# One stage's set-up loads, the last softmax denominators and a first pair of inputs placed elsewhere in a six-stage kernel

## The chip, the cores and the metric

The kernel runs on one core of a Trainium2 chip. The core has TensorE (matrix products into PSUM), VectorE, ScalarE and GpSimd for the rest, and SyncE, which here only issues DMAs. The metric is the device time of one launch in microseconds, the median of several runs.

## The reference

The input is 16 images of 64 channels by 32x32 positions (1024 tokens each), all float32. What is computed, one step after another:

```python
# L0: transformer block per image, 8 heads of 32
qkv = layer_norm(x) @ w_qkv.T
out = softmax(q @ k.T / sqrt(32)) @ v
y   = x + out @ w_proj.T + b_proj
y   = y + relu(layer_norm(y) @ w1.T + b1) @ w2.T + b2
# L1: residual block
z   = relu(bn2(conv3x3(relu(bn1(conv3x3(y, c1))), c2)) + y)
# L2: iterative whitening over groups of 16 channels, all images together
m   = mean(z);  Sigma = EPS*I + (z-m)(z-m).T / n;  P = I
for _ in range(5): P = 1.5*P - 0.5*(P@P@P) @ (Sigma/trace(Sigma))
w   = (P / sqrt(trace(Sigma))) @ (z-m) * weight + bias
# L3: state space model over the 1024 tokens of each image
xi, gate = split(layer_norm(w) @ W_in.T)
u   = silu(causal_conv4(xi));  dt, B, C = split(u @ W_x.T)
d   = softplus(dt @ W_dt.T + b_dt)
h_t = h_{t-1} * exp(d_t * A) + d_t * u_t * B_t;   y_t = h_t . C_t
out = ((y + u*Dp) * silu(gate)) @ W_out.T + w
```

## The kernel before

The kernel is written by hand for each engine: every stage is a block with one program for each of the five engines, ordered by semaphores, and all engines meet at the end of a block. Six blocks follow one another: layer norm (`layer_norm_phase`), attention (`attention_phase`), feed-forward with the two convolutions (`feed_forward_conv_phase`), the whitening matrix (`whitening_phase`), whitening with a second layer norm (`whiten_norm_phase`), and the state space model (`state_space_phase`). Between stages the data goes through DRAM. Two images lie side by side on the 128 partitions (a pair); there are 8 pairs. Each stage has its own SBUF tiles, given back when it ends, and so each loads its own weights, columns of biases and small constant matrices at its start. A column of biases (`for_both_images`) is 64 numbers read twice, one number for each partition.

Layer norm has two rounds of four pairs. SP loads the pairs (line 69) and is done with that when the last buffer of the second round is free; GpSimd stores the results (line 141) and waits for the last store.

Attention goes through 32 groups (16 images by 2 groups of four heads), each in two halves of 512 queries. A half has eight steps, one for each block of 128 keys (`KB` = 8): TensorE makes the scores of four heads (lines 416 and 423), ScalarE takes the exponentials into `probs` (line 527), TensorE multiplies the block before with the values into `O` (`values`, line 435). The denominators are sums of `probs` over the keys. They go another way: SP copies key block 1 into `odd_sums` (`copy_block`, line 306), GpSimd adds blocks 0, 2, 4, 6, 7 in place (`add_even`, line 615) and has accumulating DMAs add blocks 3 and 5 (`add_odd`, line 607) and then the one sum to the other (`add_sums`, line 622), and TensorE adds up the 128 partitions with a matrix of ones (`denominator`, line 408). For all but the last half this is done one half later, in step 14 or 6 of the next one (`extra`). ScalarE takes the reciprocal as Ln and Exp (lines 498, 502) and copies `O` into `att` (line 491), GpSimd multiplies the two (`normalise`, line 627), SP stores (line 298). Behind the last half the same steps stand by themselves, one after another. While a group runs, TensorE and VectorE also make the row maxima of the next one (lines 356, 565); the last group (`"last"`) has none of these to make. `image(b, stage)` is SP's program for one image.

The feed-forward stage runs pairs through a software pipeline. On SP `load(0, 0)` brings the attention output and the input of pair 0 (lines 745, 747) behind two matrices, then come the other weights (lines 751 to 756) and `load(0, 1)`. GpSimd issues the DMAs of 14 columns (lines 991, 993) and clears two padded buffers (line 995). ScalarE and VectorE make the batch-norm factors `bn` from those columns, and only then does ScalarE raise `c1_done`, on which TensorE's first `project` (line 788) waits.

Whitening loads three matrices and waits for them before its first product (line 1051). The stage after it loads four columns and a matrix and waits for all five before its first product (line 1214). The state space stage clears `xn`, loads the first image (line 1352), then eleven constants (lines 1364 to 1374), and waits for all before it makes the combined tap weights (from line 1431 on) and the first convolution (line 1449).

Of the kernel before, what the change touches and what calls it, by code (L numbers as in the profile page):

```python
# [36 lines left out]
def layer_norm_phase(nc, sem, x_d, gain, shift, mean_m, out_d):  # L37
# [3 lines left out]
    with ExitStack() as ctx:  # L41
# [23 lines left out]
        def _(sp):  # L65
# [10 lines left out]
            with sp.Fori(1, ROUNDS) as i:  # L76
                for u in range(FLIGHT):
                    load(i, u)

# [68 lines left out]
def attention_phase(nc, sem, xn_d, wqkvT, ident_bf, attn_d):  # L148
# [65 lines left out]
    def same_bank_before(stage, grp, unit):  # L214
# [8 lines left out]
        return was, grp - 1, [u for u in UNITS[was] if u[3] == unit[3]][-1]  # L223

    with ExitStack() as ctx:
# [61 lines left out]
        def _(sp):  # L287
# [20 lines left out]
            def image(b, stage):  # L308
# [13 lines left out]
                copy_block(b, 1, 1)  # L322
# [4 lines left out]
            with sp.Fori(0, 2) as i:  # L327
                for n in range(NB // 2 - 1):
                    image((NB // 2 - 1) * i + 1 + n, "mid")
            image(NB - 1, "last")  # L330
# [5 lines left out]
        def _(pe):  # L336
# [73 lines left out]

            def scores(stage, grp, par, s):
# [30 lines left out]
            def period(grp, par, stage):  # L442
                for s in range(STEPS):
# [34 lines left out]
        def _(act):  # L478
# [30 lines left out]
            def period(grp, par, stage):  # L509
# [42 lines left out]
        def _(dve):  # L552
# [30 lines left out]
            def period(grp, par, stage):  # L583
                for s in range(STEPS):
# [13 lines left out]
        def _(pool):  # L598
# [30 lines left out]
            def period(grp, par, stage):  # L629
                for half in range(2):  # L630
                    add_even(grp, half, 0)
# [8 lines left out]
                if stage == "last":  # L640
                    normalise(grp, 1)
# [4 lines left out]
def feed_forward_conv_phase(nc, sem, attn_d, x_d, wpT, b_proj, g2, beta2, w1T, b1, w2T, b2, mean_m,  # L646
                            c1, bn1, c2, bn2, out_d, total):

    ROUNDS = PAIRS // 2
    FF = w1T.shape[1]
    M = FF // P  # L660
    PADDED = IMG + 2
    KH = 3
    with ExitStack() as ctx:
        sb = lambda name, shape, dt=F32: ctx.enter_context(nc.sbuf_tensor(name, shape, dt))
        mm = sb("fc_mm", [P, P])
        wp = sb("fc_wp", [P, GROUPS, C])
        w1 = sb("fc_w1", [P, 2, FF])
        w2 = sb("fc_w2", [P, M, C])
        cw = sb("fc_cw", [P, 2, 2 * KH, C])
        cols = sb("fc_cols", [P, 12])  # L670
        b1c = sb("fc_b1c", [P, M])
# [1130 lines left out]
```

## Time and profile before

| | us |
|---|---|
| median of 3 runs | 3499.21 (3495.88 to 3499.93) |
| the profiled execution's own time | 3492.03 |
| its span, first to last instruction | 3490.3 |
| layer norm | 0 to 54.2 |
| attention | 54.2 to 1816.0 |
| feed-forward and convolutions | 1816.0 to 2189.2 |
| whitening matrix | 2189.2 to 2253.7 |
| whitening and norm | 2253.7 to 2328.0 |
| state space | 2328.0 to 3490.3 |

The stages are read off the timeline: each starts where the first DMA or table load of its block is issued. Times inside the kernel count from the span's start. In a row, the second number of a merged piece runs from its first to its last instruction; `[13.75 <-DMA t]` says that the engine had been idle for 13.75 us and what ended it.

### The profile page before, as it was taken

The page shows a single profiled execution, that of the slowest core. Times are in us where ns is not written, and L with a number is a line of the kernel's source. Part 1 is how long each engine was busy: PE and PEld are TensorE (multiplying, and loading weights), DVE is VectorE, ACT ScalarE, POOL GpSimd, SP SyncE. Part 2 cuts the span into 40 slices and gives each one's busy share as a digit, 9 for nine tenths or more (in the row PEclk, how much of TensorE's full clock was granted, in tenths as well). Part 3 has the DMA queues.
Part 4 walks back from the last instruction along what each step waited for, and adds up shares of the span by engine and source line. Part 5 has one row for each costly group of instructions (what it writes and reads, how often), then busy time and mean ns, then how long its engine had stood idle before and what let it go on. Part 6 is the DMA issues. An engine that isn't in the chain of part 4 may idle for free. (4 is left out here: it accounts for less than half of the span.)

```text
span 3490.3 us, 54609 instructions
## 1 busy us (share of the span) xinstructions
PE 3056.1 (88%) x17526; PEld 1156.3 (33%) x17526; DVE 2526.1 (72%) x3282; ACT 2045.6 (59%) x2445; POOL 2163.6 (62%) x876
## 2 busy tenths in 40 slices
PE   5999999999999999999957999556887788877877
PEld 2333333333333333333312333422232222222222
DVE  4888888888788888888812221236898889898888
ACT  3577777777677777777732332235556545655554
POOL 0588888888778888888870000016666766676665
PEclk7899999999999999999979999778999999999999
DMA  3577777777767777777763210134343434434343
GB/s 108 121 170 173 185 170 178 184 172 172 172 168 177 176 179 172 176 185 173 170 149 111 94 42 12 63 116 152 124 154 126 146 129 143 146 127 163 109 158 121
DMA packets 111603, 503.25 MB, mean 144 GB/s; under 512 B 17184, under 2 KB 18276, under 8 KB 78516
## 3 DMA queue, kind: packets, MB, share of 16 engines
q0 software_dynamic: 32704, 218.17, 29.9%
q1 hardware_dynamic: 78676, 282.17, 23.5%
q8 instruction: 132, 2.16, 0.2%
q14 instruction: 91, 0.75, 0.1%
HBM read 192.42 MB, written 39.39 MB: 66 GB/s over the span
## 5 line engine op out<-in xcount | busy, mean ns | idle before, releaser
L565 DVE TENSOR_REDUCE at_pmax<-at_ring 128x1 f32<-128x512 f32 x2048 | 1289.2, 685 | 280.2 <-PE at_ring L356 279.0
L527 ACT ACTIVATE at_probs<-at_sc 128x1024 f32<-128x1024 f32 x1024 | 992.5, 1021 | 371.1 <-PE at_sc L423 369.6
L615 POOL TENSOR_TENSOR at_prob_sums<-at_prob_sums,at_probs 128x2048 f32<-128x2048 f32 x192 | 907.1, 4725 | 72.2 <-ACT at_probs L527 71.9
L416 PE MATMUL at_sc<-at_QT,at_KT 32*128 32x512 f32 x4096 | 774.4, 632 | 8.3 <-issue 7.1
L1695 POOL TENSOR_TENSOR ss_drive<-ss_du,ss_bsb 128x1024 f32<-128x1024 f32 x261 | 610.7, 2353 | 263.4 <-DVE ss_state L1652 256.6
L1595 ACT ACTIVATE ss_decay<-ss_delta,ss_a 128x512 f32<-128x512 f32 x520 | 354.5, 687 | 446.9 <-DVE ss_state L1648 298.9
L435 PE MATMUL at_O<-at_probs,at_V 128*32 128x512 f32 x4096 | 536.2, 607 | 1.1 <-ACT at_probs L527 1.1
L1484 PE MATMUL ss_Y<-ss_seen,ss_ident 128*128 128x512 f32 x1032 | 520.1, 628 | 0.0
L356 PE MATMUL at_ring<-at_KH,at_QH 32*128 32x512 bf16 x2048 | 430.1, 387 | 6.9 <-DVE at_pmax L565 4.0
L1660 DVE TENSOR_TENSOR ss_seen<-ss_state,ss_C 128x1024 f32<-128x1024 f32 x259 | 316.3, 1221 | 78.7 <-PE ss_C L1472 70.8
L1652 DVE TENSOR_TENSOR_SCAN ss_state<-ss_decay,ss_state,ss_drive 128x512 f32<-128x512 f32 x259 | 332.3, 1283 | 33.6
L615 POOL TENSOR_TENSOR at_prob_sums<-at_probs 128x2048 f32<-128x2048 f32 x64 | 299.0, 4671 | 88.0 <-ACT at_probs L527 87.7
L1648 DVE TENSOR_TENSOR_SCAN ss_state<-ss_decay,ss_drive 128x512 f32<-128x512 f32 x259 | 314.9, 1216 | 32.2 <-POOL ss_drive L1695 16.5
L1472 PE MATMUL ss_C<-ss_bc,ss_select 96*128 96x512 bf16 x518 | 160.8, 393 | 191.6 <-DVE ss_seen L1660 191.2
L356 PEld LDWEIGHTS at_ring<-at_KH,at_QH 32*128 32x128 bf16 x2048 | 145.9, 92 | 523.8 <-DVE at_pmax L565 374.6
L423 PE MATMUL at_sc<-at_nrow,at_ones_bf 1*128 1x512 bf16 x2048 | 315.6, 379 | 0.2 <-ACT at_nrow L485 0.2
L1484 PEld LDWEIGHTS ss_Y<-ss_seen,ss_ident 128*128 128x128 f32 x1032 | 201.8, 200 | 228.0 <-issue 174.9
L416 PEld LDWEIGHTS at_sc<-at_QT,at_KT 32*128 32x128 f32 x4096 | 258.6, 184 | 36.9 <-ACT at_probs L527 25.4
L999 POOL DMA_DIRECT2D scratch_x<-fc_out x8 | 4.3, 534 | 345.1 <-ACT fc_out L900 345.1
L607 POOL DMA_DIRECT2D at_odd_sums<-at_probs x128 | 120.5, 941 | 149.3 <-DMA at_odd_sums<-at_probs 95.1
L369 PE MATMUL at_ring<-at_xn,at_w 64*128 64x512 f32 x256 | 150.3, 668 | 27.0 <-DMA at_xn<-scratch_xn 19.4
L1472 PEld LDWEIGHTS ss_C<-ss_bc,ss_select 96*128 96x128 bf16 x518 | 40.4, 101 | 385.9 <-DVE ss_seen L1660 323.2
(195 smaller groups left out, 2847.7 us busy)
## 6 DMA issues: line engine op xcount, KB each, us to landing
ss_bsb<-scratch_rows SPq DMA_DIRECT2D x265, 512.0 KB, 6.9
at_odd_sums<-at_probs POOLq DMA_DIRECT2D x128, 1024.0 KB, 7.6
at_odd_sums<-at_probs SPq DMA_DIRECT2D x64, 1024.0 KB, 4.8
at_prob_sums<-at_odd_sums POOLq DMA_DIRECT2D x64, 1024.0 KB, 8.1
scratch_attn<-at_att SPq DMA_DIRECT2D x64, 256.0 KB, 2.0
fc_att<-scratch_attn SPq DMA_DIRECT2D x32, 512.0 KB, 5.8
ss_xn<-scratch_xm SPq DMA_DIRECT2D x34, 256.0 KB, 5.6
at_xn<-scratch_xn SPq DMA_DIRECT2D x32, 256.0 KB, 6.5
```

The source lines that it names most:

```text
L356: nc.tensor.matmul(ring[:, unit[3], :], QH[head(h), p, blk(quad // 2)], KH[head(h), p, hs(quad % 2)], start=True, stop=True).then_inc(max_ ...
L416: nc.tensor.matmul(sc[:, h, :], KT[head(h), par, blk(kb)], QT[head(h), par, hs(half)], start=True, stop=False)
L423: m = nc.tensor.matmul(sc[:, of, :], ones_bf[row, :], nrow[row, half, :], start=False, stop=True)
L435: m = nc.tensor.matmul(O[head(h), :], V[:, par, kb, head(h)], probs[:, kb, h, :], start=(kb == 0), stop=(kb == KB - 1))
L527: nc.scalar.activation(probs[:, kb, two, :].rearrange("p h q -> p (h q)"), sc[:, two, :].rearrange("p h q -> p (h q)"), ACT.Exp, scale=SCA ...
L565: nc.vector.tensor_reduce(pmax[:, quad // 2, h, quad % 2:quad % 2 + 1], ring[:, unit[3], :], AX_X, ALU.max, negate=True).then_inc(max_done, 1)
L615: nc.gpsimd.tensor_tensor(prob_sums[:, half, :, :], before, probs[:, POOL_ADDS[n], :, :], ALU.add).then_inc(pool_sums, 1)
L1484: m = nc.tensor.matmul(Y[:, hs(h)], ident[:], seen[:, n % DEPTH, hs(h)], start=False, stop=(n == N - 1))
L1595: nc.scalar.activation(decay[:, hs(h)], delta[:, par, hs(h)], ACT.Exp, scale=a_neg[:, n:n + 1])\
L1652: nc.vector.tensor_tensor_scan(now[:, hs(1)], decay[:, hs(1)], drive[:, n % DEPTH, hs(1)], now[:, HALF - 1:HALF], ALU.mult, ALU.add).then_ ...
L1660: nc.vector.tensor_tensor(seen[:, n % DEPTH, :], state[:, n % 2, :], Cp[:], ALU.mult).then_inc(seen_done, 1)
L1695: nc.gpsimd.tensor_tensor(drive[:, n % DEPTH, :], du[:, par, :], bsb[:, n % SLOTS, :], ALU.mult).then_inc(drive_done, 1)
```

## The change

- A new class `Constants` holds the weights, columns and matrices of all later stages in tiles that live for the whole kernel, with six semaphores. Its `load` (43 DMAs) runs on SP at the end of layer norm's SP program. The loads at the start of the four later stages are gone; their waits now name the new semaphores. Matrices that two stages use (`mean_m`, `ident`) are loaded once.
- SP, before the last image of attention, fetches pair 0 of the feed-forward stage (four DMAs of attention output and one of input, 512 KB each) into tiles of its own. The feed-forward stage begins with `load(0, 1)`.
- In the last half of attention, TensorE sums each key block of `probs` itself: four products with the ones matrix for each of 8 blocks, accumulated in a free PSUM slot (`last_denominators`), one block a step from the second step on and the last block behind the last `values`. The copy, GpSimd's four adds and the three accumulating DMAs of that half are gone, and so is the separate denominator. ScalarE's copy of `O` is gone too: VectorE multiplies `O` in PSUM with the reciprocal. GpSimd's `normalise` of the half before comes at once.
- ScalarE raises `c1_done` before it waits for the columns.

```diff
+class Constants:
+    def load(self, sp):
+        sp.dma_start(self.wp[:], a["L0_conv_w_proj"].rearrange("(g p) c -> p g c", p=P)).then_inc(self.ff_matrices, DMA)
+        sp.dma_start(self.mm[:], a["mean_m"]).then_inc(self.ff_matrices, DMA)
...
+        for n, v in enumerate(vectors):
+            sp.dma_start(self.cols[:, n:n + 1], for_both_images(v)).then_inc(self.ff_vectors, DMA)
...
+        sp.dma_start(self.select[:], a["select_m"]).then_inc(self.ss, DMA)
@@ layer_norm_phase, SP
             with sp.Fori(1, ROUNDS) as i:
                 for u in range(FLIGHT):
                     load(i, u)
+            later.load(sp)
@@ attention_phase
+    LAST_SLOT = (unit_of("last", "den", 0)[3] + 1) % SLOTS
@@ SP
-                copy_block(b, 1, 1)
+                if stage != "last":
+                    copy_block(b, 1, 1)
...
+            for half in range(2):
+                sp.wait_ge(att_stored[half], 2 * GROUPS * DMA)
+            for b in range(2):
+                for g in range(GROUPS):
+                    sp.dma_start(later.att0[:, b, g, :], av[b, g]).then_inc(later.pair0, DMA)
+            sp.dma_start(later.x0[:], x_d[0:2].rearrange("b c s -> (b c) s")).then_inc(later.pair0, DMA)
             image(NB - 1, "last")
@@ TensorE
+            def last_denominators(grp, k):
+                if k == 0:
+                    pe.wait_ge(max_done, counted_before(N_MAX, grp) + N_MAX["last"])
+                    pe.wait_ge(extra_done, unit_count("last", grp, unit_of("last", "turn", 1)))
+                for h in range(GH):
+                    m = nc.tensor.matmul(ring[head(h), LAST_SLOT, :], ones[:, head(h)], probs[:, k, h, :],
+                                         start=(k == 0), stop=(k == KB - 1))
+                if k == KB - 1:
+                    m.then_inc(extra_ready, 1)
...
+                    if stage == "last" and s > KB:
+                        last_denominators(grp, s - KB - 1)
...
                     values(stage, grp, par, 1, KB - 1)
-                    pe.wait_ge(max_done, counted_before(N_MAX, grp) + N_MAX["last"])
-                    pe.wait_ge(extra_done, counted_before(N_EXTRA, grp) + N_EXTRA["last"])
-                    denominator(0, 2 * NG - 1, 1)
+                    last_denominators(grp, KB - 1)
@@ ScalarE
-                    take_raw(grp, 1)
-                    reciprocal(0, counted_before(N_EXTRA, grp) + N_EXTRA["last"] + 1, 2 * NG - 1)
+                    reciprocal(LAST_SLOT, counted_before(N_EXTRA, grp) + N_EXTRA["last"] + 1, 2 * NG - 1)
@@ VectorE
+                if stage == "last":
+                    dve.wait_ge(pv_done, STEPS * NG)
+                    dve.wait_ge(rden_done, 2 * NG)
+                    dve.wait_ge(att_stored[1], (NG - 1) * DMA)
+                    nc.vector.tensor_tensor(att[:, 1, :], rden[:], O[:], ALU.mult).then_inc(od_free, 1)
@@ GpSimd
+                    if stage == "last" and half:
+                        normalise(grp, 0)
+                        continue
@@ feed_forward_conv_phase, SP
-            sp.dma_start(wp[:], wpT.rearrange("(g p) c -> p g c", p=P)).then_inc(first_in, DMA)
-            sp.dma_start(mm[:], mean_m).then_inc(first_in, DMA)
...
-            load(0, 0)
...
             load(0, 1)
@@ ScalarE
+            act.sem_inc(c1_done, 4)
+            act.wait_ge(later.ff_vectors, later.N_FF_VECTORS * DMA)
...
             act.wait_ge(bn_done, 2)
-            act.sem_inc(c1_done, 4)
@@ GpSimd
-            for n, v in enumerate(vectors):
-                pool.dma_start(cols[:, n:n + 1], for_both_images(v)).then_inc(vectors_in, DMA)
...
@@ whiten_norm_phase, TensorE
-            pe.wait_ge(consts_in, 5 * DMA)
@@ state_space_phase, SP
-            sp.dma_start(w_in[0:C, :], w_inT).then_inc(w_in_done, DMA)
             sp.wait_ge(cleared, 1)
             load_x(0)
-            sp.dma_start(cw[:], conv_w).then_inc(consts_in, DMA)
...
```

## Rows read from the trace of the kernel before

**Rows 1.** The page's costliest group: out<-in, count | busy us, mean ns | idle before, releaser.
```profile
L565 DVE TENSOR_REDUCE at_pmax<-at_ring 128x1 f32<-128x512 f32 x2048 | 1289.2, 685 | 280.2 <-PE at_ring L356 279.0
```
**Rows 2.** Timeline, end of attention: start, length, engine, line, operation, tiles, [idle before].
```profile
1790.24 1.94 ACT L527 ACTIVATE at_probs<-at_sc 128x1024 f32<-128x1024 f32 x2
...
1799.94 0.86 POOL L622 DMA_DIRECT2D at_prob_sums<-at_odd_sums  x1 [0.61 <-POOL at_prob_sums L615]
...
1807.04 1.94 PE L408 MATMUL at_ring<-at_prob_sums,at_ones 128*32 128x512 f32 x8 [13.75 <-DMA at_prob_sums<-at_odd_sums]
...
1810.44 1.25 POOL L627 TENSOR_TENSOR at_att<-at_att,at_rden 128x512 f32<-128x512 f32 x1 [9.64 <-ACT at_rden L502]
...
1811.72 0.33 SPq L298 DMA_DIRECT2D scratch_attn<-at_att  x1
```
**Rows 3.** Timeline, start of the feed-forward stage.
```profile
1815.99 1.28 ACT L851 ACT_TABLE_LOAD   x1 [5.70 <-PEq L225]
...
1827.08 8.04 POOL L995 MEMSET fc_pad<- 128x4624 f32 x2
...
1838.41 0.29 ACT L855 ACTIVATE fc_bn<-fc_cols,fc_eps 128x1 f32<-128x1 f32 x1 [21.14 <-DMA fc_b1c<-in_L_conv_b]
...
1840.17 5.79 PE L788 MATMUL fc_A<-fc_att,fc_wp 128*64 128x512 f32 x16 [31.20 <-ACTq L859]
```
**Rows 4.** Timeline of TensorE in the last half of attention.
```profile
1776.46 1.15 PE L416 MATMUL at_sc<-at_QT,at_KT 32*128 32x512 f32 x8
...
1777.75 1.06 PE L435 MATMUL at_O<-at_probs,at_V 128*32 128x512 f32 x8
...
1787.80 1.04 PE L408 MATMUL at_ring<-at_prob_sums,at_ones 128*32 128x512 f32 x8
1788.77 1.15 PE L416 MATMUL at_sc<-at_QT,at_KT 32*128 32x512 f32 x8
```
**Rows 5.** Windows: length, busy time and count by engine, PE clock, DMA share, GB/s.
```profile
1691.00:1717.00 26.00, 25.80 (x218) 9.83 (x216) 21.66 (x36) 19.38 (x23) 20.92 (x9) 1.00 0.71 163
...
1773.00:1777.00 4.00, 4.00 (x24) 0.92 (x26) 0.00 (x0) 1.17 (x2) 3.53 (x2) 0.59 1.06 324
...
1837.00:1844.00 7.00, 3.83 (x10) 1.39 (x12) 0.87 (x6) 0.88 (x4) 0.00 (x0) 0.50 0.97 369
```
**Rows 6.** Timeline around the half before which the change puts its fetch.
```profile
1692.95 0.47 SPq L306 DMA_DIRECT2D at_odd_sums<-at_probs  x1
...
1721.16 0.87 POOL L622 DMA_DIRECT2D at_prob_sums<-at_odd_sums  x1 [0.61 <-POOL at_prob_sums L615]
...
1733.75 1.04 PE L408 MATMUL at_ring<-at_prob_sums,at_ones 128*32 128x512 f32 x8
```
**Rows 7.** Timeline, starts of the three later stages.
```profile
2189.21 1.28 ACT L1086 ACT_TABLE_LOAD   x1 [5.86 <-PEq L663]
...
2192.15 0.59 PE L1051 MATMUL wh_small<-total,wh_pair 128*128 128x1 f32 x2 [11.40 <-DMA wh_ident<-in_ident]
...
2253.68 0.61 SPq L1192 DMA_DIRECT2D wn_cols<-in_L_conv_weight  x1
...
2259.53 9.51 PE L1214 MATMUL wn_bank<-x_centred,wm 128*128 x16 [7.32 <-DMA wn_mean_m<-in_mean_m]
...
2329.06 1.13 SPq L1352 DMA_DIRECT2D ss_xn<-scratch_xm  x2
...
2340.51 0.69 PE L1431 MATMUL ss_aux<-ss_ident,ss_w_in 64*128 64x64 f32 x2 [30.43 <-DMA ss_ident<-in_ident]
...
2345.00 6.00 PE L1449 MATMUL ss_aux<-ss_xn,ss_w_taps 128*128 128x512 f32 x8 [0.96 <-ACT ss_w_taps L1566]
```
**Rows 8.** Tile `ss_xn`, from issue to landing.
```profile
DMA to landing us min/median/max: 3.7/5.6/6.5
```
**Rows 9.** SP's timeline, its last issue in layer norm.
```profile
20.89 0.33 SPq L69 DMA_DIRECT2D ln_x<-in_x  x1
```
**Rows 10.** Tile `fc_w`, its issues on SP: ns min/median/max, first and last start.
```profile
L751 SPq DMA_DIRECT2D fc_w<-in_L_conv_w x2: 1980/2456/2933, 1823.1 to 1826.1; - x2
```

More of the change, by code:

```diff
@@ L41, in layer_norm_phase @@
+def layer_norm_phase(nc, sem, x_d, gain, shift, mean_m, out_d, later):
     with ExitStack() as ctx:
@@ L145, in _, with attention_phase @@
                         pool.sem_inc(xn_free, 2)
-def attention_phase(nc, sem, xn_d, wqkvT, ident_bf, attn_d):
+def attention_phase(nc, sem, xn_d, wqkvT, ident_bf, attn_d, x_d, later):
     NG = NB * GROUPS
@@ L639, in period, with feed_forward_conv_phase @@
                     add_sums(grp, half)
-                if stage == "last":
-                    normalise(grp, 1)
             image_loop(pool, period)
-def feed_forward_conv_phase(nc, sem, attn_d, x_d, wpT, b_proj, g2, beta2, w1T, b1, w2T, b2, mean_m,
-                            c1, bn1, c2, bn2, out_d, total):
+def feed_forward_conv_phase(nc, sem, attn_d, x_d, out_d, total, later):
     ROUNDS = PAIRS // 2
-    FF = w1T.shape[1]
-    M = FF // P
+    M = later.M
     PADDED = IMG + 2
@@ L674, in feed_forward_conv_phase @@
         acc = sb("fc_acc", [P, 2])
-        att = sb("fc_att", [P, 2, 2, GROUPS, S])
-        x = sb("fc_x", [P, 2, S])
+        att = (later.att0, sb("fc_att1", [P, 2, GROUPS, S]))
+        x = (later.x0, sb("fc_x1", [P, S]))
         y = sb("fc_y", [P, 2, S])
@@ L697, in feed_forward_conv_phase @@
                                      "conv2_done", "res_done", "out_done", "out_free", "total_done"))
-        in_sem = [sem(f"fc_in{u}") for u in range(2)]
+        in_sem = [later.pair0, sem("fc_in1")]
         stored = [sem(f"fc_stored{u}") for u in range(2)]
@@ L764, in _ @@
             pe.sem_inc(proj_done, 2)
-            pe.wait_ge(first_in, 2 * DMA)
+            pe.wait_ge(later.ff_matrices, later.N_FF_MATRICES * DMA)
             def statistics(dst, src, u, done):
@@ L842, in _ @@
                 stage(0, 0)
-            pe.wait_ge(consts_in, N_MATRICES * DMA)
             pe.wait_ge(cleared, 6)
@@ L989, in _ @@
             pool.sem_inc(out_free, 2)
-            for n, v in enumerate(vectors):
-                pool.dma_start(cols[:, n:n + 1], for_both_images(v)).then_inc(vectors_in, DMA)
-            for m in range(M):
-                pool.dma_start(b1c[:, m:m + 1], b1[m * P:(m + 1) * P].rearrange("(p o) -> p o", o=1)).then_inc(vectors_in, DMA)
             for pad in (pad1, pad2):
@@ L1001, in _, with whitening_phase @@
                     pool.sem_inc(out_free, 1)
-def whitening_phase(nc, sem, x_d, total, pair_m, mask_m, ident_m, centred, wm):
+def whitening_phase(nc, sem, x_d, total, centred, wm, later):
     NC, ITERATIONS = 16, 5
@@ L1049, in _ @@
         def _(pe):
-            pe.wait_ge(consts_in, 3 * DMA)
+            pe.wait_ge(later.whitening, later.N_WHITENING * DMA)
             nc.tensor.matmul(small[:, 0:1], pm[:], total[:], start=True, stop=True).then_inc(mean_sum, 1)
@@ L1161, in _, with whiten_norm_phase @@
             dve.wait_ge(dve_step, 10 + 4 * ITERATIONS)
-def whiten_norm_phase(nc, sem, x, wm, weight, bias, ln_w, ln_b, mean_m, xw_d, xn_d):
+def whiten_norm_phase(nc, sem, x, wm, xw_d, xn_d, later):
     ROUNDS = PAIRS // FLIGHT
@@ L1190, in _ @@
         def _(sp):
-            for n, v in enumerate((weight, bias, ln_w, ln_b)):
-                sp.dma_start(cols[:, n:n + 1], for_both_images(v)).then_inc(consts_in, DMA)
-            sp.dma_start(mm[:], mean_m).then_inc(consts_in, DMA)
             for dst in (xw_d, xn_d):
@@ L1234, in _ @@
             nc.vector.memset(eps[:], EPS).then_inc(eps_set, 1)
-            dve.wait_ge(consts_in, 5 * DMA)
+            dve.wait_ge(later.norm, later.N_NORM * DMA)
             with dve.Fori(0, ROUNDS) as i:
@@ L1427, in _ @@
         def _(pe):
-            pe.wait_ge(consts_in, 11 * DMA)
-            pe.wait_ge(w_in_done, DMA)
+            pe.wait_ge(later.ss, later.N_SS * DMA)
             nc.tensor.matmul(aux[:, 0:C], w_in[0:C, 0:DI], ident[0:C, 0:C], start=True, stop=True).then_inc(plain_ready, 1)
@@ L1568, in _ @@
                     .then_inc(taps_done, 1)
-            act.wait_ge(consts_in, 11 * DMA)
+            act.wait_ge(later.ss, later.N_SS * DMA)
             take_x(0)
@@ L1626, in _ @@
             nc.vector.memset(xn[:], 0.0).then_inc(cleared, 1)
-            dve.wait_ge(consts_in, 11 * DMA)
+            dve.wait_ge(later.ss, later.N_SS * DMA)
             dve.sem_inc(y_step, 1)
```

160 lines of the change are left out of this document (86 added, 74 removed).

## The prediction

> **What bounds the kernel now.** The profiled execution took 3492.03 us, its span is 3490.3, so 1.7 lie around it; the median of the runs is 3499.21, 7.2 above. The sum below is made against 3492.03 and the 7.2 are added at the end. A measurement of this kernel can tell about 0.2% (7 us) from no change.
>
> I read the stages off the timeline, then each seam between two stages: when the stage begins, when its first product starts, and what that product's row names as the end of its wait. Inside the long stages the change touches only the last half of attention. So the question is what stands on the path at five seams and in one half of 26 us.
>
> At the end of attention the last exponential ends at 1790.24 + 1.94 = 1792.18, but the last store is only issued at 1811.72. In between stand GpSimd's add chain up to the DMA at 1799.94, a wait of 13.75 us on TensorE for that DMA, 1.94 us of denominators, 1.46 us to the multiply on GpSimd, and 1.25 us for that [rows 2]. The next stage begins at 1815.99 and its first product at 1840.17, 24.18 us later: ScalarE had waited 21.14 us for the last column, and TensorE waits for ScalarE's `c1_done` [rows 3]. All other engines are idle there but for GpSimd's two memsets. Whitening's first product starts 2.94 us after its table load and is released by a matrix; the stage behind it waits 5.85 us (2253.68 to 2259.53) for a matrix queued behind four columns; the state space stage makes its first convolution 15.94 us after it issued its input [rows 7].
>
> **The change part by part.**
>
> *End of attention.* Removed: 1811.72 - 1792.18 = 19.54 us from the last exponential to the issue of the last store [rows 2]. In its place: the last `values` (1.06) and the last block's denominators. One set of four such products costs 1.04 [rows 4]; the row counts them as x8, so a block's four products are one such piece. Then Ln and Exp, 1.46 with the hand-offs by the old chain; then the multiply. VectorE multiplying 512 columns of PSUM is not in the trace; its row maximum over as many takes 0.685 [rows 1], GpSimd's multiply 1.25 [rows 2], and I take 0.7, the same engine and memory. Hand-offs 0.3, and `values` may start some 0.6 late, since block 6's denominators stand ahead of it in TensorE's order. Sum 0.6 + 1.06 + 1.04 + 1.46 + 0.7 + 0.3 = 5.2. Gain 14.3.
>
> *What it costs the half.* TensorE gets seven more pieces of about 1.0 in steps 9 to 15. From step 11 to step 15 scores start at 1776.46 and 1788.77, 12.31 us for four steps, 3.08 a step, of which the old denominators take 1.04 once. A step's own work is 1.29 for scores (1776.46 to 1777.75) and about 1.0 for values [rows 4], 2.3 in all; the rest is waiting for exponentials, which the new piece partly fills. With it a step is 3.3, and the one with the old denominators too 4.3: 14.2 instead of 12.3, +1.9. ScalarE's reciprocal in step 14, which held up the last exponentials by 0.8, is covered then (-0.8). Just before, from 1773 to 1777, the granted clock is 0.59 of the full 2.4 GHz, so part of the stretch ran at 1.2 GHz, after TensorE had run out of row maxima to make; that costs 4 x 0.41 = 1.6 [rows 5]. The added products fill that hole; whether the clock then stays up the trace of before cannot show, so the stretch is worth -1.6 to +2 (two new pieces at half the clock). I take +0.4. Together +1.5, bounds -0.5 to +4. The seam of attention gains 14.3 - 1.5 = 12.8.
>
> GpSimd's adds of that half and SP's copy cost nothing off the path and gain nothing.
>
> *The fetch.* Five DMAs (2.6 MB) go on SP's queue ahead of the last image's first copy. That copy is issued at 1692.95 [rows 6], when the exponentials it needs are there; SP has waited for them till then, and five issues of 0.33 [rows 2] fit. The transfers are the question. In that half the DMA engines are 0.71 busy at 163 GB/s; at their fullest they moved 369 GB/s [rows 5], so 2.6 MB are 7.1 us of all engines, and the copy, on the same queue, lands up to that much later. GpSimd's first accumulating DMA waits for the copy, and behind it in GpSimd's order stand two adds, `normalise` and the sum. Of the sum TensorE has this slack: issued 1721.16, read 1733.75, 12.6 us [rows 6] against a landing of 7.1 (1799.94 to 1807.04, [rows 2]): 5.5, of which I count 4.5, since more is in flight there. GpSimd idles some 5 us of the half (20.92 busy of 26, [rows 5]) and so absorbs part of the delay. I take +0.5, bounds 0 to +4 from 7.1 less the slack, with a point for a second victim.
>
> The Trainium skill, "DMA: Bandwidth & Descriptors", section "Issuing engines are not separate DMA queues", says that DMAs from all engines run on the same 16 DMA engines and interleave, so GpSimd's accumulating DMAs would be slowed too, not only the copy on SP. Rows 5 agree in so far as both kinds make up the 0.71.
>
> *Start of the feed-forward stage.* Everything that the first product reads is there; what it still waits for is ScalarE's `c1_done`, behind a table load of 1.28 [rows 3]. So it starts 1.4 after the stage's start instead of 24.18: gain 22.8. What may be late next: the batch-norm factors, 1.8 us from ScalarE's first step to the product (1838.41 to 1840.17), now beside the product; and GpSimd's memsets of 8.04 [rows 3], which stood behind the 14 columns and now begin at once. What they clear is waited for behind the product (5.79) and the chain of five passes over 1024 columns to the normalised pair, each over 1 us by twice the 0.685 of [rows 1]: 1.4 + 5.79 + 5 = 12, so they stay covered. The clock is low before and after: 5.79 for the first product either way. An unseen wait for instructions could appear; bounds 20 to 23.
>
> *The three later seams.* Whitening: 2.94 becomes about 0.3, gain 2.6. The next: the product still waits for ScalarE's `ln_done`, behind the table load, 1.4 in place of 5.85: gain 4.4. State space: issue of the input stays where it is (it waits for a memset). It lands 0.6 (second issue) + 5.6 [rows 8] = 6.2 later; the tap weights took 4.5 from their first product (2340.51 to 2345.00) and stay under it. So 15.94 - 6.2 = 9.7; with a landing of 3.7 it is 11.6, with 6.5 it is 8.8 [rows 7, 8]. The rows' landings are mostly from the loop, with more in flight, so I take 4.6 and 10.7. Together 17.7, bounds 14 to 19.
>
> *The 43 loads.* SP has nothing to issue from 21.2 [rows 9] to the seam at 54.2, 33 us, less the 1 it needs at the barrier. A column of this form on SP's queue took 0.61 to issue [rows 7], and there are 16; the plain ones lie between 0.33 [rows 2] and, behind full queues, 2.93 [rows 10]. 16 x 0.61 + 27 x 0.6 = 26 us: covered. With the two first weight matrices at 2.9 each and 0.9 for the columns it is 35, +3. I take +0.5, bounds 0 to +6, also for layer norm's last stores, which share the engines.
>
> The Trainium skill, same page, "Rules for kernel authors", speaks against these columns: an outermost dimension of two copies keeps a DMA on at most two engines, and transfers under 64 KB are mostly overhead. Here 14 columns, issued by GpSimd, were in at 1838.41, 22.4 us after the stage began [rows 3], with all other loads of the stage beside them; 16 at that pace are 26 us, inside the 33.
>
> *Sum.* -12.8 + 0.5 - 22.8 - 17.7 + 0.5 = -52.3. 3492.0 - 52.3 = 3439.7; in the frame of the median 3446.9. I forecast **3447**.
>
> **The rivals.**
>
> (a) *The fetch holds up attention.* The sums of two halves come late: the one issued beside the fetch and the one behind the copy. Each reaches TensorE 7.1 - 4.5 = 2.6 late, and the delay is not made up: about +5 to +8, 3454. For it: DMA 0.71 busy. Against: GpSimd's idle time.
>
> (b) *The added products run at the lower clock.* If the clock falls as at 1773 in most of the half, eight pieces cost 1.0 more each: +8, 3455. Against: they make TensorE busier.
>
> (c) *SP is late at layer norm's end*: 43 loads at 0.9, 39 us, +6: 3453.
>
> (d) *The seams keep another wait.* The first products find something the rows hide behind the DMA wait, such as code not yet fetched; it costs some 3 to 5 us at each of four seams, half of the gain at the two big ones at most: +15, 3462.
>
> (e) *Slower: the 43 loads stop SP.* All issues on SP are in order and attention cannot begin before the last one. If each went at the pace of the weights behind a full queue, 2.93 at most [rows 10], SP would end at 21.2 + 126 = 147 and attention begin 94 us late: 3447 + 94 = 3541. It decides from a pace of (32 + 52.3)/43 = 2.0 us a load on. For it: two of the rows 10 pace are among them. Against: those stood behind 2.6 MB, and the column on SP took 0.61.
>
> (f) *It doesn't do what it says*: the seams wait as long, because the new semaphores are reached as late as the old; that would need the loads to be in flight 1750 us after their issue. Less than 1%.
>
> **How the numbers follow.** Forecast 0.57; (a) 0.13, (b) 0.09, (c) 0.10, (d) 0.07; (e) 0.02; between them a loss of some 46 us from several of these, within 0.2%: 0.02. Faster 0.96, same 0.02, slower 0.02. The range: the sum's better ends (12.8 + 2, 23, 19, no other cost) give -57, 3442; a run in the frame of the profiled execution is a few us lower, so 3438. Upwards (a), (b) and (c) one at a time reach 3455 and the bounds of two terms together 3461; (d) and (e) are left out.
>
> **What would show it.** Attention's last store issued about 5 us after the last exponential, and that exponential 1 to 2 us later in its half; the feed-forward stage's first product 1.4 after its table load; 0.3, 1.4 and some 5 at the other seams; layer norm's length unchanged at 54.2; TensorE's read of the sum at its place in the half of the fetch. The prediction is wrong if a seam keeps its length with another releaser, if the last half grows by more than 4 us, or if attention begins after 60.

## The result and the profile after

| | before | after |
|---|---|---|
| median, us | 3497.55 (3493.19 to 3499.93) | 3446.18 (3440.86 to 3447.96) |
| profiled execution, us | 3492.03 | 3445.46 |
| ratio | | 0.9852 (0.984 to 0.9864) |

The change saves 51.4 us in the medians and 46.6 in the two profiled executions. By stage, in the profiled ones (a stage of after starts with its first instruction of any engine, since with the loads gone its first DMA or table load can come up to 1.2 us later):

| stage | before | after | difference | forecast |
|---|---|---|---|---|
| layer norm | 54.2 | 53.5 | -0.7 | +0.5 |
| attention | 1761.8 | 1754.2 | -7.6 | -12.3 |
| feed-forward | 373.2 | 354.2 | -19.0 | -22.8 |
| whitening matrix | 64.5 | 62.3 | -2.2 | -2.6 |
| whitening and norm | 74.3 | 69.8 | -4.5 | -4.4 |
| state space | 1162.3 | 1149.8 | -12.5 | -10.7 |
| sum | | | -46.5 | -52.3 |

**End of attention** (timeline of after; it answers to [rows 2]). The last exponentials end at 1800.08 + 1.02 = 1801.10, the last store is issued at 1805.21: 4.1 us where 19.54 were. What is left is values, one block of denominators, Ln, Exp and VectorE's multiply of 0.69.

```profile
1800.08 1.02 ACT L620 ACTIVATE at_probs<-at_sc 128x1024 f32<-128x1024 f32 x1
1801.15 1.07 PE L528 MATMUL at_O<-at_probs,at_V 128*32 128x512 f32 x8 [0.24 <-ACT at_probs L620]
1802.04 1.04 PE L499 MATMUL at_ring<-at_probs,at_ones 128*32 128x512 f32 x8
1803.14 0.60 ACT L591 ACTIVATE at_lden<-at_ring 128x512 f32<-128x512 f32 x1 [2.04 <-PE at_ring L499]
1803.77 0.63 ACT L595 ACTIVATE at_rden<-at_lden 128x512 f32<-128x512 f32 x1
1804.49 0.69 DVE L690 TENSOR_TENSOR at_att<-at_rden,at_O 128x512 f32<-128x512 f32 x1 [39.12 <-ACT at_rden L595]
1805.21 0.33 SPq L373 DMA_DIRECT2D scratch_attn<-at_att  x1
1807.72 1.28 ACT L917 ACT_TABLE_LOAD   x1 [3.32 <-PEq L300]
```

**The half of the fetch** (timeline of after, then two windows with the columns of [rows 5], then two windows of before that lie as far behind the same store, then the landings of tile `at_odd_sums` in after; before: [rows 6]).

```profile
1693.00 1.80 SPq L411 DMA_DIRECT2D k_att<-scratch_attn  x4
1694.84 0.57 SPq L412 DMA_DIRECT2D k_x<-in_x  x1
1695.62 0.48 SPq L381 DMA_DIRECT2D at_odd_sums<-at_probs  x1
...
1711.45 0.88 POOL L704 DMA_DIRECT2D at_odd_sums<-at_probs  x1 [8.10 <-ACT at_probs L620]
...
1732.42 0.88 POOL L719 DMA_DIRECT2D at_prob_sums<-at_odd_sums  x1 [0.61 <-POOL at_prob_sums L712]
...
1740.35 1.94 PE L491 MATMUL at_ring<-at_prob_sums,at_ones 128*32 128x512 f32 x8 [3.74 <-DMA at_prob_sums<-at_odd_sums]
...
1696.00:1702.00 6.00, 5.80 (x52) 1.83 (x46) 5.09 (x10) 4.03 (x6) 4.73 (x3) 1.00 1.01 358
1702.00:1708.00 6.00, 6.00 (x52) 2.00 (x52) 4.92 (x9) 4.12 (x6) 1.35 (x1) 1.00 1.04 289
...
1693.00:1699.00 6.00, 5.80 (x50) 2.01 (x44) 5.11 (x9) 4.03 (x6) 4.37 (x3) 1.00 0.88 259
1699.00:1705.00 6.00, 6.00 (x53) 2.03 (x56) 4.99 (x9) 4.11 (x5) 3.78 (x3) 1.00 0.98 199
...
DMA to landing us min/median/max: 4.4/7.4/15.3
```

The DMA engines are full for 12 us. Before, they were nearly full there too, at fewer GB/s (0.88 and 0.98 busy), which the mean of 0.71 over the half hides. The copy issued at 1695.62 takes 15.3 us to land (5.2 before), GpSimd stands 8.10 us ahead of its accumulating DMA (1.35 us busy in the second window; the row names the exponentials, but the copy that it also waits for landed at 1695.62 + 15.3 = 1710.9), and TensorE now waits 3.74 us for the sum, for which it had not waited before. Behind that wait its granted clock is 0.50, and the product that waited takes 1.94 us instead of 1.04.

**Start of the feed-forward stage** (TensorE's timeline of after, its first three windows of 7 us, and the same three windows of before; before: [rows 3]). The first product starts 1.43 us after the table load, as forecast. But it takes 6.51 us, not 5.79, the third piece 3.62, where before it took 1.98, and the first two hidden products 3.75 and 2.98 (before 3.59 and 1.88): the granted clock of these stretches is 0.58, 0.90 and 0.74, where before it was 0.69, 1.00 and 0.79.

```profile
1809.15 6.51 PE L855 MATMUL fc_A<-k_att,k_wp 128*64 128x512 f32 x16 [6.07 <-ACT L917]
...
1821.58 3.62 PE L836 MATMUL fc_A<-fc_sq,k_mm 128*128 128x512 f32 x4 [2.46 <-ACT fc_sq L929]
1829.68 3.75 PE L875 MATMUL fc_B<-fc_yn,k_w 128*128 128x512 f32 x4 [4.49 <-DVE fc_yn L1011]
1833.23 2.98 PE L875 MATMUL fc_A<-fc_yn,k_w 128*128 128x512 f32 x4
1836.04 1.88 PE L875 MATMUL fc_B<-fc_yn,k_w 128*128 128x512 f32 x4
...
1809.12:1816.12 7.00, 6.51 (x16) 1.94 (x16) 1.36 (x9) 0.78 (x4) 6.51 (x2) 0.58 0.99 346
1816.12:1823.12 7.00, 3.53 (x6) 1.36 (x7) 2.17 (x2) 1.06 (x1) 0.00 (x0) 0.90 0.74 232
1823.12:1830.12 7.00, 2.51 (x4) 0.80 (x3) 2.04 (x2) 2.17 (x2) 0.00 (x0) 0.74 0.40 164
...
1840.14:1847.14 7.00, 5.79 (x16) 1.73 (x16) 1.05 (x1) 0.00 (x0) 0.00 (x0) 0.69 0.53 214
1847.14:1854.14 7.00, 3.97 (x8) 1.35 (x8) 1.45 (x2) 1.36 (x2) 0.00 (x0) 1.00 0.77 265
1854.14:1861.14 7.00, 2.85 (x4) 1.33 (x5) 2.04 (x2) 1.86 (x2) 0.00 (x0) 0.79 0.28 112
```

**Later seams and layer norm's end** (timeline of after; before: [rows 7, 9]). Two of the first products start with their stage, the convolution 6.0 us after its own. SP's last load ends at 51.88, and attention begins at 53.53.

```profile
51.44 0.44 SPq L105 DMA_DIRECT2D k_select<-in_select_m  x1
53.53 1.14 SPq L364 DMA_DIRECT2D at_w<-in_L_conv_w_qkv  x2
...
2161.97 0.56 PE L1108 MATMUL wh_small<-total,k_pair 128*128 128x1 f32 x2 [7.37 <-PEq L750]
...
2224.18 1.28 ACT L1271 ACT_TABLE_LOAD   x1 [20.14 <-PEq L1071]
...
2224.57 2.07 PE L1266 MATMUL wn_bank<-x_centred,wm 128*128 x2 [1.86 <-ACTq L1273]
...
2293.93 0.66 PE L1456 MATMUL ss_aux<-k_ident,k_w_in 64*128 64x64 f32 x2 [17.04 <-PEq L1224]
...
2299.99 1.22 PE L1474 MATMUL ss_aux<-ss_xn,ss_w_taps 128*128 128x512 f32 x1 [1.95 <-DMA ss_xn<-scratch_xm]
```

### The profile page after: what moved, and what is told of

Its sections match the earlier page's. It is cut to its first block and busy times, and to the rows that moved or that the text cites. A ratio compares the mean times of both kernels' runs of the same rounds, so it can differ in the third digit from the quotient of the medians.

```text
span 3443.8 us, 54701 instructions
## 1 busy us (share of the span) xinstructions
PE 3065.5 (89%) x17582; PEld 1159.7 (34%) x17582; DVE 2526.9 (73%) x3283; ACT 2045.1 (59%) x2444; POOL 2132.9 (62%) x854
## 5 line engine op out<-in xcount | busy, mean ns | idle before, releaser
L712 POOL TENSOR_TENSOR at_prob_sums<-at_prob_sums,at_probs 128x2048 f32<-128x2048 f32 x189 | 891.0, 4714 | 70.0 <-ACT at_probs L620 69.6
L1620 ACT ACTIVATE ss_decay<-ss_delta,k_a 128x512 f32<-128x512 f32 x520 | 354.5, 687 | 446.7 <-DVE ss_state L1673 298.7
L1509 PE MATMUL ss_Y<-ss_seen,k_ident 128*128 128x512 f32 x1032 | 520.1, 628 | 0.0
L1497 PE MATMUL ss_C<-ss_bc,k_select 96*128 96x512 bf16 x518 | 160.7, 393 | 191.6 <-DVE ss_seen L1685 191.2
L1509 PEld LDWEIGHTS ss_Y<-ss_seen,k_ident 128*128 128x128 f32 x1032 | 201.7, 200 | 227.9 <-issue 173.1
L1497 PEld LDWEIGHTS ss_C<-ss_bc,k_select 96*128 96x128 bf16 x518 | 40.4, 101 | 385.9 <-DVE ss_seen L1685 323.1
```

Source lines behind the costliest of these rows:

```text
L712: nc.gpsimd.tensor_tensor(prob_sums[:, half, :, :], before, probs[:, POOL_ADDS[n], :, :], ALU.add).then_inc(pool_sums, 1)
L1509: m = nc.tensor.matmul(Y[:, hs(h)], ident[:], seen[:, n % DEPTH, hs(h)], start=False, stop=(n == N - 1))
L1620: nc.scalar.activation(decay[:, hs(h)], delta[:, par, hs(h)], ACT.Exp, scale=a_neg[:, n:n + 1])\
```

## The experiments

Times are medians; the ratio is to the kernel before on the same chip. In all that follows "stretch" is the time from the issue of the store ahead of the last image (1692.41 in after) to the first exponential of the last half (1774.46): 77.09 before, 82.05 after. "Late fetch" is the third experiment, the base of all behind it but the old denominators, whose base is after.

**No fetch.** The five DMAs go back to the start of the feed-forward stage.

```diff
-            for b in range(2):
-                for g in range(GROUPS):
-                    sp.dma_start(later.att0[:, b, g, :], av[b, g]).then_inc(later.pair0, DMA)
-            sp.dma_start(later.x0[:], ...).then_inc(later.pair0, DMA)
...
+            load(0, 0)
             load(0, 1)
```

> The changed kernel without the fetch in attention; pair 0 is loaded at the start of the feed-forward stage, ahead of pair 1. If the fetch is what makes TensorE wait 3.7 us for the sum of the half behind it, the stretch from the store before the fetch to the first exponential of the last half is 77.1 us again, as before the change, instead of 82.1. The first product of the feed-forward stage then waits for 2.6 MB: 7.1 us at 369 GB/s and 2 to 3 of latency, so it starts some 9.5 after the stage's start instead of 1.4. Together +3: 3449. Rival, the stretch is longer for another reason (the profiled execution, the tiles' places): it stays at 82 and the time is 3454.

3447.4 us (3442.36 to 3448.08), 0.9852 (0.9835 to 0.9868). The stretch is 77.27, as before the change: the fetch did cost the 5 us. The first product starts 9.6 us after the stage's start, held by `k_x`:

```profile
1811.96 6.10 PE L849 MATMUL fc_A<-k_att,k_wp 128*64 128x512 f32 x16 [14.25 <-DMA k_x<-in_x]
```

So in its place the fetch gained 8.2 at the one end and lost 5.0 at the other; the medians with it and without it (3446.18 and 3447.4) can't be told apart.

**Fetch behind the copy.** The same five DMAs, issued right behind the first copy of the last image.

```diff
                 copy_block(b, 0, 0)
+                if stage == "last":
+                    fetch()
...
```

> The fetch one step later on SP: behind the last image's first copy instead of ahead of it. If the delay comes from the order on SP's queue (the copy lands 15.3 us after its issue because 2.6 MB stand ahead of it), the copy lands in about 5, GpSimd's first accumulating DMA is not held up, the stretch is 77 to 78 and the time 3441. If it comes from the shared DMA engines, the accumulating DMAs land late in its place, GpSimd's chain is late all the same, the stretch is 80 to 82 and the time 3444 to 3446.

3439.34 us (3432.64 to 3440.03), 0.9827 (0.981 to 0.9843); the stretch is 81.12, so going behind the copy took back only 1 us of the 5. The copy now lands in 5.7 us. GpSimd's timeline shows where the rest stays: its first accumulating DMA goes out in time, but lands after 16.0 us (8.3 before the change), and the second waits for it.

```profile
1721.19 0.88 POOL L708 DMA_DIRECT2D at_odd_sums<-at_probs  x1 [8.92 <-DMA at_odd_sums<-at_probs]
```

So in both places what was in flight beside the 2.6 MB was slowed, SP's copy in after and GpSimd's DMA here. The Trainium skill says in "DMA: Bandwidth & Descriptors", section "Issuing engines are not separate DMA queues", that DMAs of all issuing engines run on the same 16 DMA engines and interleave, and this row agrees (8.92 us of waiting). That the total is 7 us below that of after comes mostly from elsewhere. In the profiled runs the feed-forward stages, of the same code, differ by 5.5 us (349.0 against 354.5 from table load to table load), at granted clocks of 0.75, 1.00, 0.76 and 1.00 in the first four stretches of 7 us instead of 0.58, 0.90, 0.74 and 0.62.

**Late fetch.** The five DMAs go out behind the store of the last image's first group (`store(b, 0, 1)`), into the last half, which has no copy and no accumulating DMAs of its own any more.

```diff
                 store(b, 0, 1)
+                if stage == "last":
+                    fetch()
...
```

> The fetch in the last half of attention, behind the last image's third store, where the copy and the accumulating DMAs of that half are gone. Theory: only one accumulating DMA (the sum of the half before) is in flight beside it, and it has 14 us; the stretch is 77, the last half as in the changed kernel (24.7 from the first to the last exponential's start), the data is there before the stage starts, the time 3441. Rival: the sum lands behind the fetch, up to 7 us late, and TensorE waits 0 to 3 for it; or the fetch lands after the stage's start; time 3442 to 3446.

3437.64 us (3435.49 to 3441.54), 0.9826 (0.981 to 0.9842). The stretch is 76.75, the last half as in after (24.70), the first product 1.43 after the stage's start. The fetch has both ends of its gain here.

**Old denominators.** In after, the last half makes its denominators over SP, GpSimd and DMAs again.

```diff
-                if stage != "last":
-                    copy_block(b, 1, 1)
+                copy_block(b, 1, 1)
...
-                    last_denominators(grp, KB - 1)
+                    denominator(0, 2 * NG - 1, 1)
```

> The changed kernel with the old way of the last half's denominators: copy, GpSimd's adds, accumulating DMAs, then the separate products, and GpSimd's multiply. By the traces the new way gains 17.2 us from the last exponential's start to the stage's end and costs 0.9 in the half: without it the time is 16 longer, 3462. The prediction's terms (14.3 less 1.5) give 3459.

3461.58 us (3457.81 to 3464.21), 0.9894 (0.9878 to 0.9911): 15.4 above after. TensorE's row has its old wait again (13.75 before), in spite of everything else being changed, and the last half is back at 23.77 us from its first to its last exponential, as before (24.70 in after).

```profile
1817.27 1.94 PE L490 MATMUL at_ring<-at_prob_sums,at_ones 128*32 128x512 f32 x8 [15.75 <-DMA at_prob_sums<-at_odd_sums]
```

**TensorE kept busy.** The low clock at the start of the feed-forward stage has two possible causes: the idle time around it, or the work itself. From here on the kernel with the late fetch gets extra products whose results nobody reads, made from a constant of the state space stage; TensorE waits for that constant once, at the start of attention.

```diff
                     last_denominators(grp, KB - 1)
+                    for _ in range(18):
+                        nc.tensor.matmul(ring[:, (LAST_SLOT + 1) % SLOTS, :], ones_bf[0:96, :], later.filler, start=True, stop=True)
...
+            pe.wait_ge(later.ss, later.N_SS * DMA)
...
-            for stage in (project, means, variances):
+            fill(4)
+            for stage, n in ((project, 5), (means, 9), (variances, 16)):
                 stage(0, 0)
+                fill(n)
```

> The kernel with the late fetch (3437.6), with 52 extra bf16 products on TensorE whose results nobody reads, put where it idles: 18 behind the last denominators of attention, 4 at the start of the feed-forward stage, 5, 9 and 16 behind the first three products of pair 0. The feed-forward stage of the late fetch took 351.8, its first product 5.20 and the first two hidden products 3.75 and 3.13 against 3.6, 1.88 and 1.88 at full clock. Theory (the idle stretch at the seam lowers the granted clock, and that gave back part of the 22.8): the granted clock of the first 28 us is 1.0, these three pieces take their full-clock times, stage 346 to 348, time 3433. Rival 1 (the lower clock comes of the pair's own load, not of the idle time before): pieces as before, stage 352, time 3438. Rival 2 (the extra products stand in the way of the pair's own, because at the lower clock they outlast the gaps): stage 355 or more, time 3441 or more.

3430.1 us (3428.77 to 3432.33), 0.9811 (0.9798 to 0.9825): the lowest median of all, though the interval of its ratio overlaps that of the late fetch. The stage takes 344.0 instead of 351.8. TensorE's rows, and the window of the first product; ahead of them the first product with the late fetch, and last the final convolution of the stage, with the late fetch and here:

```profile
1804.64 5.20 PE L859 MATMUL fc_A<-k_att,k_wp 128*64 128x512 f32 x16 [6.10 <-ACT L921]
...
1802.97 3.65 PE L863 MATMUL fc_A<-k_att,k_wp 128*64 128x512 f32 x16 [0.22 <-ACT L931]
...
1819.01 1.95 PE L883 MATMUL fc_B<-fc_yn,k_w 128*128 128x512 f32 x4 [1.04 <-DVE fc_yn L1025]
...
1802.94:1809.94 7.00, 6.69 (x26) 2.47 (x27) 2.32 (x9) 0.78 (x4) 6.52 (x2) 1.00 0.97 346
...
2135.15 12.22 PE L847 MATMUL fc_B<-fc_pad,k_cw 128*64 128x512 f32 x48 [2.46 <-DVE fc_pad L1031]
...
2127.38 10.52 PE L851 MATMUL fc_B<-fc_pad,k_cw 128*64 128x512 f32 x48 [2.46 <-DVE fc_pad L1041]
```

The same product that took 5.20 to 6.59 us takes 3.65 at the full clock, granted at 1.00 through the first four stretches of 7 us. So the idle time lowers the clock, not the work. Of the 7.8 us that the stage is shorter, 4.6 lie in pair 0: its fourth hidden product starts 22.7 us after the stage's start instead of 27.2. The other 3.2 lie in the last pair, some 310 us later, where both kernels have the same code and no extra products: its two convolutions take 11.97 and 10.52 us instead of 13.53 and 12.22. That the extra products have a part in this is not shown; the clock there differs between runs without them too.

**The extra products at the seam alone**, and **in the pair alone**: two halves of the same edit, each shown against the run before.

```diff
-            for stage, n in ((project, 5), (means, 9), (variances, 16)):
+            for stage, n in ((project, 0), (means, 0), (variances, 0)):
```

> The kernel that keeps TensorE busy (3430.1, feed-forward stage 344.0 against 351.8 with the late fetch), with the extra products at the seam alone: 18 behind the last denominators and 4 at the start of the stage, none inside pair 0. If the idle 6 us of the seam lowered the clock: first product 3.65 in place of 5.20, hidden products 1.9 to 2, stage 345 to 347, time 3431. If the pair's own gaps (1.46, 2.46 and 4.49) did it: first product 3.65, but the hidden products behind the last gap 3.75 and 3.1 as with the late fetch, stage 349 to 350, time 3435.

```diff
-                    for _ in range(18):
+                    for _ in range(0):
...
-            fill(4)
```

> The other half: the extra products of pair 0 (5, 9 and 16) without those at the seam. If the seam's idle stretch lowered the clock: first product 5.2 to 6.5, then the clock comes back within the pair, since TensorE is busy, hidden products 1.9, stage 346 to 349, time 3433. If the pair's own gaps did it: only the first product is slow or not even that, stage 345 to 346, time 3431.

At the seam alone: 3435.75 us (3434.53 to 3437.38), 0.9826 (0.981 to 0.9843), stage 351.4. The first product takes 3.65, but the clock falls behind it, and what was won is lost again (the fourth hidden product starts 27.0 us into the stage):

```profile
1802.73 3.65 PE L863 MATMUL fc_A<-k_att,k_wp 128*64 128x512 f32 x16 [0.22 <-ACT L931]
1807.84 1.99 PE L844 MATMUL fc_B<-fc_y,k_mm 128*128 128x512 f32 x4 [1.46 <-DVE fc_y L1014]
1812.29 3.58 PE L844 MATMUL fc_A<-fc_sq,k_mm 128*128 128x512 f32 x4 [2.46 <-ACT fc_sq L943]
1820.36 3.75 PE L883 MATMUL fc_B<-fc_yn,k_w 128*128 128x512 f32 x4 [4.49 <-DVE fc_yn L1025]
```

In the pair alone: 3434.5 us (3431.65 to 3434.95), 0.9823 (0.9806 to 0.9839), stage 346.6. Here the first product is slow, with 0.50 granted in the 1.4 us before it, and all behind it runs at full clock:

```profile
1802.70 6.13 PE L863 MATMUL fc_A<-k_att,k_wp 128*64 128x512 f32 x16 [6.10 <-ACT L930]
...
1821.21 1.95 PE L883 MATMUL fc_B<-fc_yn,k_w 128*128 128x512 f32 x4 [1.04 <-DVE fc_yn L1024]
```

So both idle stretches lower the clock, the one of the seam for the first product, the pair's own gaps for what follows. What each is worth is not shown. The fourth hidden product starts 25.2 us into the stage here, and in the five profiles whose stage has the code of after (after, fetch behind the copy, late fetch, old denominators, sixteen more loads) anywhere from 25.8 to 30.1: only both together, at 22.7, stand well clear. The other 3.1 us of this stage's 5.2 lie in the last pair again, and the ratio is that of the late fetch. The Trainium skill, "TensorE: Matmul & The Clock Gate", section "HAM oscillation — how this bites in real kernels", tells of a kernel whose waits (there for DMAs) between bursts of products drop the clock, so that each burst starts slow; the rows at the seam alone agree, with waits of 1.46 and 2.46 us for VectorE and ScalarE ahead of a product of 3.58 us that took 1.98 with the late fetch.

**Sixteen more loads** at the end of layer norm.

```diff
+        for n in range(16):
+            sp.dma_start(self.more[:, n:n + 1], for_both_images(vectors[n % 12])).then_inc(self.norm, DMA)
...
```

> The kernel with the late fetch, with 16 more columns loaded on SP at the end of layer norm into a tile that nobody reads. Theory (SP's issues now end layer norm, with 1 us of slack at most): the columns cost 16 x 0.98 (14 of them took 13.5 us) = 15.7, attention begins 14 to 16 us later, at 69 to 71, time 3452. Rival (layer norm is still ended by its last store and the loads have room): attention begins at 55, time 3438.

3453.54 us (3448.31 to 3454.27), 0.9873 (0.9857 to 0.9888), 15.9 above the late fetch. Attention begins at 68.35 instead of 55.13, right behind SP's last load:

```profile
67.13 0.43 SPq L108 DMA_DIRECT2D k_select<-in_select_m  x1
68.35 1.14 SPq L367 DMA_DIRECT2D at_w<-in_L_conv_w_qkv  x2
```

That last load moved by 14.06 (53.07 to 67.13), 0.88 a load, and attention by 13.2: the 43 loads left about 0.8 us.

**Columns in the stage.** GpSimd issues the 14 columns at the start of the feed-forward stage, as before; `c1_done` stays early.

```diff
...
+            later.columns(pool)
             for pad in (pad1, pad2):
```

> The kernel with the late fetch, with the 14 columns issued by GpSimd at the start of the feed-forward stage as in the kernel before; everything else (weights, matrices, the early c1_done) as it was. Theory (the gain of 22.8 is of the columns being there; raising c1_done early only lets the first product run): the first product starts 1.4 after the stage's start, but the addition behind it waits for the batch-norm factors, which follow the last column at 15 to 22 us after the start instead of running at 6.7: stage 351.8 + 9 to 15, time 3447 to 3453. Rival (raising c1_done early is what gave the gain, the columns are needed later): at most +3, time 3441.

3449.0 us (3448.0 to 3449.81), 0.9863 (0.9848 to 0.9878). The first product starts at 1.4, but its reader, the addition, starts at 1818.93, 22.2 us after the stage's start, behind the last column:

```profile
1817.33 0.29 ACT L929 ACTIVATE fc_bn<-k_cols,fc_eps 128x1 f32<-128x1 f32 x1 [19.27 <-DMA k_b1c<-in_L_conv_b]
...
1818.93 1.28 DVE L1007 SCALAR_TENSOR_TENSOR fc_y<-fc_A,k_cols,k_x 128x1024 f32<-128x1024 f32 x1
```

The stage takes 371.0, 19.2 more than with the late fetch, where 9 to 15 had been expected. (The medians lie only 11.4 apart; in the profiles this run's attention is 4.5 us shorter and its state space stage 5.7, with code that is the same.) Raising `c1_done` early hides the product under the columns, and no more.

**`c1_done` late.** ScalarE raises it behind the batch-norm factors; the columns stay in layer norm.

```diff
-            act.sem_inc(c1_done, 4)
             act.wait_ge(later.ff_vectors, later.N_FF_VECTORS * DMA)
...
             act.wait_ge(bn_done, 2)
+            act.sem_inc(c1_done, 4)
```

> The kernel with the late fetch, but ScalarE raises c1_done behind the batch-norm factors as in the kernel before; the columns are loaded in layer norm. Theory (with the columns there the factors take 1.4 us): the first product starts 2.8 after the stage's start instead of 1.4, time 3439. Rival (the place of c1_done carries the gain): the product starts 10 us or more later, time 3448 or more.

3436.28 us (3433.17 to 3441.27), 0.9829 (0.9814 to 0.9844), not to be told from the late fetch. The product starts 3.05 us after the stage's start instead of 1.43. With the columns there, the place of `c1_done` is worth 1.6 us at most; the columns carry the rest.

## Why the prediction was right, and where its steps were not

The forecast of 3447 is within 1 us of the median, but its sum was 5.8 us too good against the profiled executions, for which it was made: 3439.7 against 3445.46. It was 4.7 short in attention and 3.8 in the feed-forward stage, and did better by 1.2 in layer norm and 1.5 at the later seams. That the median came out all the same is luck: the 7.2 us added for it belong to the profiled run of before; that of after lies only 0.7 below its median. The steps, one by one:

*End of attention, -14.3.* From the last exponential to the store 19.54 became 4.1: -15.4, a little better, since neither `values` started late (0.05 behind the exponential) nor did hand-offs cost 0.3. From the store to the next stage another 1.8 went (4.27 to 2.51), which the sum didn't have. With the old denominators it is 4.28, so it belongs to them; by what, stays open.

*The half, +1.5.* +0.9 from its first to its last exponential; a step with the new piece takes 3.15 to 3.45, forecast 3.3, and no dip of the clock is left in TensorE's rows there. Rival (b) did not come.

*The fetch, +0.5, bounds 0 to +4.* This step failed: +5.0, outside its bounds, and rival (a) is what happened in this stretch, at its lower end, though with one late sum and not two: TensorE waited only for the one behind the copy, and its clock fell in that wait. Of its numbers the slack was right: from the issue of the sum to the read 12.6 became 7.9, so 4.7 where 4.5 was counted. The delay was not. The 7.1 us took the DMA engines for the fetch alone, at their fullest pace, while the half's own copies and accumulating DMAs shared them. The 0.71 that the step went by is a mean; where the fetch was put the engines were 0.88 and 0.98 busy before it came. So the first accumulating DMA was 7.8 late against the store ahead of it (11.25 to 19.04), the sum 8.2 (31.78 to 40.01). And none of that was absorbed: from that DMA to the sum GpSimd takes 20.5 before and 21.0 after. The second accumulating DMA can go out only when the first has landed, 8.3 us after its issue before and 8.6 after, so GpSimd's idle time ahead of it could not take up the delay.

*Start of the feed-forward stage, -22.8.* The first product is 22.75 earlier, as the step said. But the stage won only 19.0: the first product took 6.51 and not 5.79, the products behind it were slower too, and 3.7 us went back. The sentence that "the clock is low before and after: 5.79 for the first product either way" is right in that the product is slow either way, and wrong in giving the clock one price: the five profiles of this code have stages of 349.0 to 354.6 us, 18.6 to 24.2 below the one profile of before, with the forecast inside. So the 3.7 are not shown to be the price of the shorter wait. The step looked at where the product starts, not at the clock under the next 28 us; the runs with extra products show that 4.6 us more were to be had in pair 0.

*Later seams, -17.7.* -19.2; the state space stage did better by 1.8. Its first convolution follows the issue of the input by 4.9 us, forecast 5.2; the other 1.5 were not traced. Rival (d) did not come: no other wait stood behind the ones removed. No run takes these seams apart; their rows carry this step alone.

*The 43 loads, +0.5.* No time was lost, but nearly (attention began at 53.53; with the same 43 loads it began at 53.7 to 55.4 in the other runs, 54.2 before): issued from 20.13 to 51.88, 31.75 us and not 26. The 0.61 for each column was mis-sized: the first twelve took 12.5 us, 1.04 each. The bound of 35 would have been a loss. Rival (c) missed by 0.8 us: sixteen loads more cost nearly their full time. Rival (e) would have wanted 2.0 us a load, and it was 31.75 / 43 = 0.74.

*Not in the sum.* Up to the store ahead of the fetch, attention is 3.7 us longer. The windows of TensorE 892 us into the stage show where, first after, then before:

```profile
945.53:955.53 10.00, 7.43 (x30) 2.62 (x34) 2.04 (x4) 2.51 (x4) 4.71 (x2) 0.50 0.54 122
955.53:965.53 10.00, 10.00 (x52) 3.99 (x50) 5.69 (x9) 5.59 (x8) 0.24 (x1) 0.53 0.35 121
```

```profile
946.23:956.23 10.00, 6.69 (x24) 1.92 (x24) 1.98 (x3) 1.94 (x2) 5.41 (x3) 0.53 0.48 112
956.23:966.23 10.00, 9.80 (x80) 4.47 (x76) 8.00 (x13) 7.38 (x10) 3.08 (x1) 0.96 0.42 134
```

TensorE idles there for some 7 us in both, and its clock halves; in after it comes back later (0.53 against 0.96 in the second window). Attention's code up to there is the same in all eleven profiles of the changed kernels, but for that one wait at its start in three, and 32 stores into attention they fall into two groups: against before, five lose 3.8 to 4.1 us at this place, six lose 1.0 or less. So when the clock returns differs from run to run. But that is not all of it: five of those six are some 2 us behind before from the first store on. The 55th store comes 1532.0 us into attention before, at 1531.8 in the run with the columns in the stage, and at 1534.0 to 1536.3 in the ten others. With a single profile of before, whether the change itself makes this part of attention some 2 us longer stays open.

## What to carry over

A seam between two stages is worth its whole length when the constants are there early; price it by the first product's start, and then look at the granted clock under that product too: behind 6 us or more without work TensorE took 5.20 to 6.59 us here for what takes 3.65. A transfer that is "hidden" under a busy half shares the DMA engines with that half, and here it cost 5.0 us on the chain of small DMAs that used them: look at their share where the transfer goes and not at a mean, and move it to a half that has no DMAs to wait for. When many small loads are put into an idle queue, their sum decides, and here the issue times of the same form on the same queue differed by more than a factor of three (0.51 to 1.84).

## What was not expected of the hardware

TensorE's granted clock falls inside a stage that seems busy: in a pair with gaps of 1.46, 2.46 and 4.49 us, products of 1.88 us lasted 3.75, and filling these gaps and the seam ahead of them with products that nobody reads won 4.6 us there. When the clock comes back isn't the same in each run of the same code (stages of 349.0 to 354.6), and this alone makes differences of several microseconds between profiles, as much as some of the steps judged here.

One column of 128 numbers took SP 0.51 to 1.84 us to issue; what makes the one slow and the other not stays open.
